# Graph part of a fused layer computed transposed, one batch at a time, with float32r parts as stationary operands

## The reference

```python
def L0(x, adj_mx, alpha_train, w, d, fc_in_w, fc_in_b):          # graph part
    h = jnp.einsum('bnd,ed->bne', x, fc_in_w) + fc_in_b
    alph = jax.nn.sigmoid(alpha_train)[:, None]
    w_eff = w * jnp.clip(d, 0.0, 1.0) @ w.T
    def euler_step(h, _):                                        # 8 steps, dt = 1/8
        ax = jnp.einsum('nm,bmd->bnd', adj_mx, h)
        f = alph * 0.5 * (ax - h) + h @ w_eff - h + x
        return (h + dt * f, None)
    ...
x = layernorm(x + L0(x, adj, ...))
qkv = x @ W                                                      # 4 heads of 32
scores = einsum('bhid,bhjd->bhij', q, k) / sqrt(32) + mask       # mask: -inf where adj == 0
out = einsum('bhij,bhjd->bhid', softmax(scores), v)
x = layernorm(x + out)
```

## Time and profile before

| | |
|---|---|
| median of 3 runs | 730.89 us (730.54 to 733.96) |
| the profiled execution | 731.09 us; its span, first to last instruction, 729.2 us |
| TensorE busy | 683.0 us (94%), its weight loads 557.5 us (76%) |
| VectorE busy | 416.7 us (57%) |
| ScalarE busy | 379.1 us (52%) |
| GpSimd busy | 71.1 us (10%) |
| mean granted TensorE clock | 0.983 of full speed |

### The profile page before, as it was taken

How to read it: one execution, slowest core, us unless ns; L and a number is a source line. 1 busy time by engine, 2 the same in 40 slices (tenths; PEclk the granted TensorE clock), 3 DMA queues, 4 the chain that set the end, 5 groups by cost and what they waited for, 6 DMA issues and landing times.

```text
span 729.2 us, 14091 instructions
## 1 busy us (share of the span) xinstructions
PE 683.0 (94%) x4753; PEld 557.5 (76%) x4753; DVE 416.7 (57%) x1229; ACT 379.1 (52%) x855; POOL 71.1 (10%) x85
## 2 busy tenths in 40 slices
...
GB/s 104 1 0 30 1 30 80 18 78 30 88 16 66 65 53 47 36 94 19 82 0 101 29 90 11 72 58 57 44 40 62 28 76 13 90 33 69 78 25 29
DMA packets 37058, 35.39 MB, mean 49 GB/s; under 512 B 7456, under 2 KB 24224, under 8 KB 37024
## 3 DMA queue, kind: packets, MB, share of 16 engines
...
## 4 chain that ended last, share of the span: by engine, by line
PE 74%; DVE 7%; issue 6%; SPq 6%; DMA 4%; ACT 2%; DVEq 0%; POOLq 0%; POOL 0%; ACTq 0%
PE psL L614 12%; PE psE L714 11%; PE psO L725 8%; PE psS L654 7%; SPq L345 5%; PE psL L625 4%; PE psL L626 4%; PE psL L627 4%; DMA Ks<-kl 4%; PE psL L644 4%; PE psL L642 4%; PE psL L643 4%; PE psM L691 3%; DVE Sm L855 2%; PE psS L559 2%
## 5 line engine op out<-in xcount | busy, mean ns | idle before, releaser
L466 ACT ACTIVATE E<-Sm,negmax 128x512 f32<-128x512 f32 x256 | 182.9, 716 | 140.1 <-DVE negmax L855 140.1
L855 DVE CUSTOM_DVE_ANT_0 Sm<-psS,mask 128x512 f32<-128x512 f32 x256 | 166.3, 684 | 16.5 <-PE psS L654 12.0
L886 DVE COPY ET<-psE 128x512 f32<-128x512 f32 x116 | 79.7, 687 | 143.8 <-PE psE L714 143.7
L614 PE MATMUL psL<-R,zT 128*128 128x128 f32 x1152 | 142.1, 275 | 0.0
L614 PEld LDWEIGHTS psL<-R,zT 128*128 128x128 f32 x1152 | 137.0, 192 | 2.0 <-issue 0.2
L714 PEld LDWEIGHTS psE<-ident,E 128*128 128x128 f32 x928 | 104.3, 141 | 36.7 <-issue 30.1
L714 PE MATMUL psE<-ident,E 128*128 128x128 f32 x928 | 122.8, 275 | 3.2 <-DVE ET L886 2.3
L654 PE MATMUL psS<-Ks,Qs 96*128 96x512 f32 x256 | 97.3, 455 | 19.4 <-DMA Ks<-kl 9.3
L514 ACT ACTIVATE ET<-psE 128x512 f32<-128x512 f32 x116 | 68.8, 593 | 58.9 <-PE psE L714 58.6
L400 POOL TENSOR_TENSOR rstd<-var,minus_half 128x4 f32<-128x4 f32 x32 | 32.3, 1009 | 568.1 <-DVE var L838 568.1
L642 PE MATMUL psL<-Yh,PTh 128*128 128x256 f32 x256 | 72.8, 284 | 0.0
...
## 6 DMA issues: line engine op xcount, KB each, us to landing
Qs<-qh SPq DMA_DIRECT2D x128, 64.0 KB, 2.0
Ks<-kh SPq DMA_DIRECT2D x128, 64.0 KB, 2.0
...
```

Of the source, the lines that this page charges most:

```text
L466: nc.scalar.activation(E[:, h % 2, i, :], Sm[:, i % 2, :], ACT.Exp, scale=-1.0, bias=negmax[:, h * NT + i:h * NT + i + 1], accum_out=sums[ ...
L614: last = mm(bank_ap[:, (t * GB + b) * D:(t * GB + b + 1) * D], zT[:, i, b, nodes], R[:, block * PW + i, :], start=False, stop=alone and t ...
L855: V_.tensor_tensor_reduce(out=Sm[:, i % 2, :], in0=psS[i % 2][:, :], in1=mask[:, i, :], scale=-SCALE, scalar=3e38, op0=ALU.add, op1=ALU.mi ...
L886: V_.tensor_copy(ET[:, n, i, :], e_bank(horner, i)[:, :]).then_inc(t_ev[1], 1)
```

## The change

The graph part is kept transposed (features on partitions, nodes along the 512 columns) and runs one batch at a time, the same pieces in every iteration. x and its powers are split into zh and zl by ScalarE and VectorE; R is split into Rh and Rl in setup. A block of coefficients is 10 matmuls of 512 columns with rb, Rh or Rl as the stationary operand and Wst, zh or zl moving. Block 2 (piece C 2) ends in bank psL1, is copied to YT and transposed back (piece YT 0) so that its high and low parts, Yh and Yl, can be the stationary operand of the join J 0, in which the power (PTh, PTl) moves. C 1 is summed into the bank of J 0. The same again gives YT 1, C 0 and J 1; the result is copied to YT, transposed (UT) and copied to u. A batch is prepared one iteration after its graph work instead of two (PREP, ATT, END = 1, 2, 3), so there are 19 iterations: 16 with graph work and 3 without.

```diff
-PREP = IPG
-ATT = IPG + 1
-END = IPG + 2
...
-U_X, U_Z, U_C = 0, GB, PW * GB
-U_B = U_C + UPS
-UPG = U_B + (BLK - 1) * UPS
-EPB = UPG // 2
...
+PREP, ATT, END = 1, 2, 3
+
+
+L0_UNITS = (("XT", 0), ("Z", 1), ("Z", 2), ("C", 2), ("YT", 0), ("J", 0), ("YT", 1), ("J", 1), ("UT", 0))
+L0_BANK = (0, 1, 0, 1, 1, 0, 0, 1, 0)
+L0_SPLIT = (("XT", 0), ("Z", 1), ("Z", 2), ("YT", 0), ("YT", 1))
+UPB = len(L0_UNITS)
+HPB = len(L0_SPLIT)
+EPB = (L0_BANK.count(0), L0_BANK.count(1))
 
 
 EVENTS = [
-    ("HORNER", 0, 0), ("PV", 0, 0), ("PV", 1, 0), ("PV", 2, 0), ("PV", 3, 0),
-    ("TR", 0, 0), ("TR", 0, 1), ("S", 1, 0), ("S", 1, 1), ("LN1A", 0, 0),
+    ("HORNER", 0, 0), ("PV", 0, 0), ("PV", 1, 0), ("PV", 2, 0), ("PV", 3, 0), ("LN1A", 0, 0),
     ("HORNER", 1, 0),
-    ("TR", 0, 2), ("TR", 0, 3), ("S", 1, 2), ("S", 1, 3), ("OT", 0, 0), ("LN1B", 0, 0),
+    ("TR", 0, 0), ("TR", 0, 1), ("S", 1, 0), ("S", 1, 1), ("OT", 0, 0),
     ("HORNER", 2, 0),
+    ("TR", 0, 2), ("TR", 0, 3), ("S", 1, 2), ("S", 1, 3), ("LN1B", 0, 0),
+    ("HORNER", 3, 0),
     ("TR", 1, 0), ("TR", 1, 1), ("S", 2, 0), ("S", 2, 1), ("CB", 0, 0),
-    ("HORNER", 3, 0), ("X1T", 0, 0),
+    ("HORNER", 4, 0), ("X1T", 0, 0),
     ("TR", 1, 2), ("TR", 1, 3), ("S", 2, 2), ("S", 2, 3), ("LN2A", 0, 0),
-    ("HORNER", 4, 0), ("Q", 1, 0), ("QL", 1, 0),
+    ("HORNER", 5, 0), ("Q", 1, 0), ("QL", 1, 0),
     ("TR", 2, 0), ("TR", 2, 1), ("S", 3, 0), ("S", 3, 1), ("LN2B", 0, 0),
-    ("HORNER", 5, 0), ("K", 2, 0), ("KL", 2, 0),
-    ("TR", 2, 2), ("TR", 2, 3), ("S", 3, 2), ("S", 3, 3),
-    ("HORNER", 6, 0),
+    ("HORNER", 6, 0), ("K", 2, 0), ("KL", 2, 0),
+    ("HORNER", 7, 0),
+    ("TR", 2, 2), ("TR", 2, 3), ("S", 3, 2), ("S", 3, 3), ("V", 3, 0),
+    ("HORNER", 8, 0),
     ("TR", 3, 0), ("TR", 3, 1), ("S0", 0, 0), ("S0", 0, 1),
-    ("HORNER", 7, 0), ("V", 3, 0),
     ("TR", 3, 2), ("TR", 3, 3), ("S0", 0, 2), ("S0", 0, 3),
-    ("HORNER", 8, 0),
+    ("HORNER", 9, 0),
 ]
...
 HORNER = [
-    [[("XT", 0)], [("XT", 1), ("Z", 0)], [("Z", 1)], [("Z", 2)], [("Z", 3)],
-     [("C", 0)], [("C", 1)], [], [("BC", 0)]],
-    [[], [("BM", 0)], [("BC", 1)], [("BM", 1)], [("BC", 2), ("XS", 0), ("XS", 1)], [("BM", 2)],
-     [("BC", 3)], [], [("BM", 3)]],
+    [("XT", 0), ("Z", 1)], [("Z", 2)], [("C", 2)], [("C", 1)], [("YT", 0)], [("XS", 0), ("J", 0)], [("C", 0)],
+    [("YT", 1)], [("J", 1)], [("UT", 0)],
 ]
...
 def run_iterations(eng, iteration):
 
-    for j in range(IPG):
-        iteration(0, j, True, False, False, False)
-    for j in range(IPG):
-        iteration(1, j, True, True, j > 0, False)
+    iteration(0, 0, True, False, False, False)
+    iteration(0, 1, True, True, False, False)
+    iteration(1, 0, True, True, True, False)
+    iteration(1, 1, True, True, True, True)
     with eng.Fori(2, NG - 1) as g:
         for j in range(IPG):
             iteration(g, j, True, True, True, True)
     for j in range(IPG):
         iteration(NG - 1, j, True, True, True, True)
-    for j in range(IPG):
-        iteration(NG, j, False, True, True, True)
-    iteration(NG + 1, 0, False, False, True, True)
-    iteration(NG + 1, 1, False, False, False, True)
+    iteration(NG, 0, False, True, True, True)
+    iteration(NG, 1, False, False, True, True)
+    iteration(NG + 1, 0, False, False, False, True)
 
...
+                        if not (is_last(g) and j == 1):
+                            split_x(1 - j, g + j + 1)
+                    elif (kind, n) in L0_SPLIT:
+                        act.wait_ge(l0_mm, l0_unit(it, (kind, n)) + 1)
+                        bank = psL[L0_BANK[L0_UNITS.index((kind, n))]]
+                        if kind == "YT":
+                            high(bank[:, :].rearrange("p (t d) -> p t d", d=D), Yh[:, :, :]).then_inc(l0_hi, 1)
                         else:
-                            if not isinstance(g, int) or g > 0:
-                                act.wait_ge(x1_done, g * GB)
-                            nc.scalar.activation(u[:, units(n % UPS), :], psL[n % 2][:, :],
-                                                 ACT.Copy).then_inc(l0_ev[n % 2], 1)
+                            high(bank[:, :], zh[:, n, :]).then_inc(l0_hi, 1)
+                    elif (kind, n) in L0_UNITS:
+                        act.wait_ge(l0_mm, l0_unit(it, (kind, n)) + 1)
+                        bank = L0_BANK[L0_UNITS.index((kind, n))]
+                        if kind == "UT":
+                            if not isinstance(it, int) or it > 0:
+                                act.wait_ge(x1_done, it)
+                            dst = u[:, :, :].rearrange("p t d -> p (t d)")
+                        else:
+                            dst = YT[:, :]
+                        nc.scalar.activation(dst, psL[bank][:, :], ACT.Copy).then_inc(l0_ev[bank], 1)
...
             pe.wait_ge(in_qkv, 16)
-            pe.wait_ge(rt_ev, 3)
...
+            def coefficients(it, block):
+
+                bank = psL[1 if block != 1 else 0][:, :]
+                mm(bank, rb[0:3 * QUAD, block, :], Wst[0:3 * QUAD, :], start=True, stop=False)
+                for i in range(PW):
+                    k = block * PW + i
+                    if block == BLK - 1 and i == PW - 1:
+                        pe.wait_ge(l0_ev[0], l0_free(it, 0, 2))
+                    mm(bank, Rh[:, k, :], zh[:, i, :], start=False, stop=False)
+                    mm(bank, Rh[:, k, :], zl[:, i, :], start=False, stop=False)
+                    last = mm(bank, Rl[:, k, :], zh[:, i, :], start=False, stop=block == BLK - 1 and i == PW - 1)
                 return last
 
...
+            def apply_power(bank, high, low, i, fresh):
+
                 for k in range(NT):
-                    mm(psL[n % 2][:, :], Xh[:, b, k, :], PTh[:, power_, k, :], start=k == 0, stop=False)
-                    mm(psL[n % 2][:, :], Xh[:, b, k, :], PTl[:, power_, k, :], start=False, stop=False)
-                    last = mm(psL[n % 2][:, :], Xl[:, b, k, :], PTh[:, power_, k, :],
-                              start=False, stop=k == NT - 1)
-                last.then_inc(l0_mm, 1)
-
...
                     if kind == "XT":
-                        if n == 0:
-                            pe.wait_ge(xin_in, 16 * (g + 1))
-                        next_unit(g, U_X + n)
+                        pe.wait_ge(xin_in[j], 16 * (g + 1))
+                        if not isinstance(it, int) or it > 0:
+                            pe.wait_ge(l0_ev[0], l0_free(it, 0, 0))
                         for t in range(NT):
-                            last = nc.tensor.transpose(psL[n % 2][:, t * P:(t + 1) * P],
-                                                       xin[:, n, t, :], ident[:, :])
+                            last = nc.tensor.transpose(psL[0][:, t * P:(t + 1) * P], xin[:, j, t, :], ident[:, :])
                         last.then_inc(l0_mm, 1)
                     elif kind == "Z":
-                        powers_of_x(g, n)
+                        if n == 1:
+                            pe.wait_ge(x_split, it + 1)
+                            if not isinstance(it, int) or it > 0:
+                                pe.wait_ge(l0_ev[1], l0_free(it, 1, 0))
+                        else:
+                            pe.wait_ge(l0_ev[0], l0_free(it, 0, 1))
+                        apply_power(psL[n % 2], Xh, Xl, n - 1, True).then_inc(l0_mm, 1)
...
+                    elif kind == "J":
+                        if n == 0:
+                            pe.wait_ge(l0_ev[1], l0_free(it, 1, 3))
+                        else:
+                            pe.wait_ge(l0_ev[0], l0_free(it, 0, 4))
+                        if isinstance(it, int) and it == 0:
+                            pe.wait_ge(pt_lo, PW * NT)
+                        apply_power(psL[n], Yh, Yl, PW - 1, False).then_inc(l0_mm, 1)
+                    elif kind in ("YT", "UT"):
+                        if kind == "UT":
+                            pe.wait_ge(l0_ev[1], l0_free(it, 1, 4))
+                        elif n == 0:
+                            pe.wait_ge(l0_ev[1], l0_free(it, 1, 2))
+                        else:
+                            pe.wait_ge(l0_ev[0], l0_free(it, 0, 3))
+                        bank = psL[L0_BANK[L0_UNITS.index((kind, n))]]
+                        for t in range(NT):
+                            nodes = slice(t * P, (t + 1) * P)
+                            last = nc.tensor.transpose(bank[:, nodes], YT[:, nodes], ident[:, :])
...
             V_.tensor_scalar(mask[:, :, :], adj_sb, 0.0, NEG, ALU.is_equal, ALU.mult).then_inc(c_vec, 1)
             dve.wait_ge(c_vec, 5)
-            dve.wait_ge(rt_ev, 3)
+            for c in range(3):
+                q0, q1 = 4 * c, min(4 * c + 4, RS)
+                dve.wait_ge(rt_hi, c + 1)
+                V_.tensor_tensor(Rl[:, q0:q1, :], R_BANKS[c][:, 0:(q1 - q0) * D].rearrange("p (q d) -> p q d", d=D),
+                                 f(Rh[:, q0:q1, :]), ALU.subtract).then_inc(rt_lo, 1)
```

(71 more changed lines are left out.)

105 lines of the change are left out of this document (38 added, 67 removed).

## The result

The changed kernel takes 803.99 us (median of 4 runs, 802.23 to 805.58), the kernel before 732.39 us in the same comparison: a ratio of 1.098, 95% interval 1.094 to 1.102. The forecast was 787 us, with a range of 750 to 822.

A forecast was written before the change was run, and what follows sets the result against it. TensorE's own in-order work was taken as the bound, so new waits count in full: 13 full iterations at 43.1 us plus setup and ends made 780.4, clock falls added 7, giving 787 us, range 750 to 822.

The forecast's parts named there:

- TensorE's work and Ks: Full iteration: TensorE's work falls 0.46 us and the wait for Ks 0.3, from 39.39 to 38.6 us.
- The wait at XT: Iteration end: XT waits 2.8 us for UT's bank, because ScalarE's copy to u stands behind the last exponentials.
- the lower bound: At XT: even with ScalarE free, waiting for the bank that UT filled would cost 0.85 us.
- The wait at J 0: Join J 0 waits 1.2 us for Yl of YT 0, since ScalarE is still busy with exponentials.
- The pace of VectorE: Last two pairs of scores, with only two TR between them: VectorE is slower than TensorE, costing 0.5 us.
- The clock: TensorE's clock falls at half of the 14 places where XT waits, 1.0 us each, 7 us in all.
- Rival (b): The clock falls at each of 14 places, costing 2.3 us each: 812 us, up to 822; chance 0.14.
- The rest: Setup and ends: first XT at 57.2 us, first three iterations 24.9, 30.2 and 39.5, stages without graph work 67.0.
- the four waits: First iteration: both joins wait 1.55 us each behind their transposes, UT and XT 0.85 each behind their copies.
- (a): The main case, with the waits and clock falls as forecast: 765 to 805 us; chance 0.68.
- The other side: Whole kernel: the change would be faster if waits stayed below 1.4 us an iteration; faster had chance 0.06.
- rival (d): Whole kernel: the copies keep up and nothing waits, giving 709 us, 3% faster; chance 0.06.

The follow-up runs named there:

- runs 1 and 5: Two separate edits to the changed kernel: PV put ahead of the next XT, 760.35 us; UT put ahead of the last scores, 749.32 us.
- run 8: Changed kernel with PV ahead of XT, YT 0 earlier, V between the last scores and a later store, plus Rl made earlier in setup with split waits: 732.12 us.
- the last run: Kernel with all earlier order, store and setup edits, plus UT and TR ahead of the last scores, then YT 1 ahead of K: 727.32 us, ratio 0.994.

## Why the prediction held, step by step

**TensorE's work and Ks.** Forecast 38.6 us an iteration without new waits. Taking the waits and the clock from the measured 44.5: 44.5 - 2.62 - 1.20 - 0.69 - 0.38 - 1.45 = 38.2. The price of the matmuls with Rh (0.234) was right, the sum 0.4 too high. The wait for Ks before was under-read. The wait list has 0.4 us an iteration, but it counts from the end of the transposes as the profile gives it. By starts, in the kernel before:

```profile
269.63 1.09 PE L714 MATMUL psE<-ident,E 128*128 128x128 f32 x8
...
308.66 1.09 PE L714 MATMUL psE<-ident,E 128*128 128x128 f32 x8
310.37 0.72 PE L654 MATMUL psS<-Ks,Qs 96*128 96x512 f32 x2 [0.62 <-DMA Ks<-kl]
```

S0 starts 1.33 (270.96) and 1.71 us behind the TR ahead of it, where TR takes 0.79: 0.54 and 0.92, or 0.73 an iteration. So 39.39 - 0.73 = 38.66 were TensorE's work before, and 38.2 after it is a gain of 0.5, as the forecast had it (0.46). The 0.4 us too much are the wait for Ks: 0.73 went, where 0.3 was taken off.

**The wait at XT.** Forecast 2.8, measured 2.62. The mechanism, ScalarE's order behind one bank, is shown by ScalarE's rows, by the run in which only UT moved, and by the first iteration, where the bank alone costs 1.0 (the lower bound was 0.85). That bound holds only while XT stands right behind UT: with other work between them (runs 1 and 5) the bank costs nothing.

**The wait at J 0.** Forecast 1.2, measured 1.20. The 0.38 us ahead of TR was missing: I priced the place behind YT 0 only, not the exponentials that TR itself waits for. Before, a Z or a unit of 2.8 to 3.1 us stood there, now C 1 with 2.34.

**The pace of VectorE.** Forecast 0.5, measured 0.69. But the reading "a cost of its own" was wrong: V between the scores gave nothing, the time turned up at XT and J 1. I had written that J 1 would wait 0.6 without V, and did not use it when I expected a gain from moving V.

**The clock.** The mis-sized term. Forecast a fall at half of the 14 places and 1.0 us each, 7 us in all; it fell at all 14, for 1.45 us each, 20 us. Rival (b) was right on how often, and wrong on the price of 2.3.

**The rest.** First XT at 57.38 (57.2), the first iteration 26.61 (24.9), the second 30.38 (30.2), the third 40.72 (39.5), the part behind 734.22 67.9 (67.0). The first stands at a clock of 0.94; run 8 has it at 26.15 and 1.00, so 0.5 of its 1.7 us is clock. Most of the rest can be read there: Z and the joins take 2.9 us each and not 2.8 (0.4), Z 2 waits 0.5 for the parts in its bank, which the sum left out, and the four waits that it did have are 5.0 and not 4.8. The miss of 17 us is 13 x 0.95 = 12 in the full iterations (a forecast of 43.1 + 0.5 against 44.55: 0.95 more for the clock, 0.4 ahead of TR, 0.2 in pace, less 0.2 at XT and 0.4 for Ks) and 4 to 5 at the ends. 803.99 lies just under the 805 of (a), and it needed some luck: the 0.4 ahead of TR, which the sum left out, and the 0.4 of Ks, which it kept, cancel. Without the second the forecast would have been 782.

The other side needed waits under 1.4 us an iteration, and the last run reached it: 39.3 us are 1.1 above the 38.2 of work, and the kernel is 4.8 us below the one before. It is not the 22 us of rival (d), which ends 18 us lower: 13 iterations at 39.3 and not at 38.6 are 9 us, and the first two (26.1 and 27.5, where (d) had 20.1 and 24.2) another 9, less the 4 by which setup is shorter; 3 to 4 us more were not traced.
